# Transformer tower on one core: GpSimd adds two or three times in turn, VectorE sums eight or four numbers, and GpSimd scales the probabilities

## The reference, cut to what matters

```python
def one_query(qs):
    return -jnp.sum(jnp.abs(qs[:, None, :, :] - k), axis=-1) * scale   # sum over 64 numbers
...
a = _l1_scores(q, k)                                  # b x 128 x 128 x 8 heads
a = jnp.concatenate([a, jnp.zeros((b, 1, t, h), a.dtype)], axis=1)
a = jax.nn.softmax(a, axis=1)[:, :t]
bf = jnp.einsum('bsdh,bshw->bdhw', a, vf)
bb = jnp.einsum('bdsh,bshw->bdhw', a, vb)
```

## Time and profile before

| | |
|---|---|
| median of 3 runs | 3506.68 us |
| time of the profiled execution | 3508.91 us |
| its span | 3507.0 us |
| PE busy | 3243.3 us (92%) |
| DVE busy | 3086.9 us (88%) |
| POOL busy | 2856.5 us (81%) |
| ACT busy | 2723.1 us (78%) |
| DMA queue of GpSimd | 501.51 MB, 72.0% of 16 engines |

### The profile page before, as it was taken

How to read it: one execution, slowest core, us unless ns; L and a number is a source line. 1 busy time by engine, 2 the same in 40 slices (tenths; PEclk the granted TensorE clock), 3 DMA queues, 4 the chain that set the end, 5 groups by cost and what they waited for, 6 DMA issues and landing times. The chain is left out here.

```text
span 3507.0 us, 78749 instructions
## 1 busy us (share of the span) xinstructions
PE 3243.3 (92%) x23140; PEld 2458.9 (70%) x23140; DVE 3086.9 (88%) x4389; ACT 2723.1 (78%) x4859; POOL 2856.5 (81%) x2792
## 2 busy tenths in 40 slices
PE   8899999999999999999999999999999999999888
PEld 6676777776777777677767777766777777777555
DVE  5888889998898989988999889989989999989886
ACT  3777787887787877877788878778778788777875
POOL 2888888888888888888888888878888888888885
PEclk8999999999999999999999999999999999999999
DMA  6778777787787787777888877877777887778884
GB/s 135 154 153 164 155 155 153 157 162 156 151 163 154 157 161 158 158 150 153 161 160 159 160 153 156 164 149 157 157 155 157 166 159 157 154 158 160 163 159 86
DMA packets 199653, 543.63 MB, mean 155 GB/s; under 512 B 69142, under 2 KB 133398, under 8 KB 146744
## 3 DMA queue, kind: packets, MB, share of 16 engines
q0 software_dynamic: 73728, 501.51, 72.0%
q1 hardware_dynamic: 125880, 41.54, 5.9%
HBM read 10.93 MB, written 2.10 MB: 4 GB/s over the span
## 5 line engine op out<-in xcount | busy, mean ns | idle before, releaser
L925 DVE TENSOR_REDUCE S<-psU 128x16 f32<-128x1024 f32 x2183 | 2604.4, 1217 | 297.8 <-PE psU L486 281.3
L486 PE MATMUL psU<-flat,kT 99*128 99x256 bf16 x16384 | 2304.1, 275 | 212.5 <-ACT absd L711 102.9
L711 ACT ACTIVATE absd<-psU 128x1024 f32<-128x1024 f32 x1913 | 1936.7, 1023 | 554.3 <-PE psU L486 541.0
L486 PEld LDWEIGHTS psU<-flat,kT 99*128 99x128 bf16 x16384 | 1495.6, 98 | 855.2 <-DVE S L925 219.3
L1194 POOL TENSOR_TENSOR absd<-absd 128x1024 f32<-128x1024 f32 (+2 forms) x512 | 1179.8, 2304 | 248.9 <-DMA absd<-absd 245.0
L1198 POOL TENSOR_TENSOR absd<-absd 128x512 f32<-128x512 f32 (+2 forms) x512 | 610.3, 1192 | 40.2
L1183 POOL DMA_DIRECT2D absd<-absd x512 | 454.2, 887 | 200.4 <-ACT absd L711 145.2
L1201 POOL TENSOR_TENSOR absd<-absd 128x256 f32<-128x256 f32 (+2 forms) x512 | 351.7, 687 | 40.1
L498 PE MATMUL psC<-c1in,w 128*128 128x384 f32 (+1 forms) x930 | 309.4, 415 | 0.8 <-DVE c1in L969 0.8
L590 PE MATMUL psZ<-P,v 128*128 128x256 f32 x1024 | 288.6, 384 | 0.0
L517 PE MATMUL psC<-c3in,w 128*128 128x128 f32 x1240 | 251.8, 287 | 1.7 <-DVE c3in L969 1.7
(11 more groups left out here) (180 smaller groups left out, 2231.3 us busy)
## 6 DMA issues: line engine op xcount, KB each, us to landing
absd<-absd POOLq DMA_DIRECT2D x412, 1024.0 KB, 7.9
absd<-absd POOLq DMA_DIRECT2D x65, 768.0 KB, 6.5
flat<-qparts SPq DMA_DIRECT2D x3072, 8.0 KB, 4.1
absd<-absd POOLq DMA_DIRECT2D x35, 512.0 KB, 4.9
xin<-in_x SPq DMA_DIRECT2D x32, 192.0 KB, 8.0
flat<-pattern SPq DMA_DIRECT2D x4, 768.0 KB, 10.9
out_h<-result SPq DMA_DIRECT2D x32, 64.0 KB, 6.0
w<-in_w SPq DMA_DIRECT2D x1, 1280.0 KB
```

What stands on the lines that cost most here:

```text
L486: mm = nc.tensor.matmul(psU[:, slot % PLACES, m], kT[0:ROWS + 3, b, m, :], flat[0:ROWS + 3, half % HALVES, :, lo:lo + BLOCK], start=True, ...
L711: nc.scalar.activation(absd[:, c % GROUPS, :, u], psU[:, slot % PLACES].rearrange("p (n a) s w -> p n (a s w)", n=2), ACT.Abs).then_inc(a_ ...
L925: nc.vector.tensor_reduce(S[:, b, hd, SB * c:SB * c + SB], psU[:, slot % PLACES].rearrange("p a s w -> p s a w"), AX.XY, ALU.add, apply_ab ...
```

## The change

`LEVELS` becomes a list: even chunks keep three adds on GpSimd, odd chunks get two. `WIDTH` follows: VectorE's last adds of an odd chunk sum 8 numbers in place of 4. The waits on `a_tree` count the adds before a chunk (`LEVELS_BEFORE`). The eight scalings of an image leave ScalarE; in their place GpSimd has two `tensor_tensor` multiplications, each over four heads (512 numbers for each partition), with `rden` broadcast. They stand in the first slot and the middle slot of what the scalings had (`spread(..., 2)`): slots 100 and 103 for the first image, 29 and 35 for the second. The transposes wait for GpSimd's semaphore `at_pool`. `SHARED` and all slot tables stay as they are.

```diff
-LEVELS = 3
-WIDTH = 4
+LEVELS = [3, 2] * CHUNKS
+LEVELS_BEFORE = [sum(LEVELS[:c]) for c in range(TREES + 1)]
+WIDTH = [BLOCK >> (n - 1) for n in LEVELS]
...
+AT_POOL = Steps("scalea scaleb")
...
-                            pe.wait_ge(at_act, AT_ACT.after(g, ("scale3", "scale7")[n]))
+                            pe.wait_ge(at_pool, AT_POOL.after(g, ("scalea", "scaleb")[n]))
...
-                for n in spread(slot, AT_AT[b]["scale"], AT_AT[b]["scale_len"], HEADS):
-                    if n == 0:
-                        act.wait_ge(at_dve, AT_DVE.after(g, "rden"))
-                    nc.scalar.activation(P[:, n, 0, :], P[:, n, 0, :], ACT.Copy, scale=rden[:, n:n + 1]).then_inc(at_act, 1)
...
-                dve.wait_ge(a_tree, LEVELS * (TREES * i + slot // HEADS + 1))
+                dve.wait_ge(a_tree, LEVELS_BEFORE[TREES] * i + LEVELS_BEFORE[slot // HEADS + 1])
...
-                                        .rearrange("p u (s w) -> p u s w", w=BLOCK)[:, :, :, 0:WIDTH],
+                                        .rearrange("p u (s w) -> p u s w", w=BLOCK)[:, :, :, 0:WIDTH[slot // HEADS]],
...
-                pool.wait_ge(a_tree, LEVELS * (TREES * i + c) + 2)
-                lo, hi = rows[:, :, :, 0:WIDTH], rows[:, :, :, WIDTH:2 * WIDTH]
-                nc.gpsimd.tensor_tensor(lo, lo, hi, ALU.add).then_inc(a_tree, 1)
+                for k in range(1, LEVELS[c]):
+                    width = BLOCK >> k
+                    pool.wait_ge(a_tree, before + k)
+                    lo, hi = rows[:, :, :, 0:width], rows[:, :, :, width:2 * width]
+                    nc.gpsimd.tensor_tensor(lo, lo, hi, ALU.add).then_inc(a_tree, 1)
...
+            def attend(p, b, slot):
+                g = 2 * p + b
+                for n in spread(slot, AT_AT[b]["scale"], AT_AT[b]["scale_len"], 2):
+                    pool.wait_ge(at_dve, AT_DVE.after(g, "rden"))
+                    heads = slice(4 * n, 4 * n + 4)
+                    nc.gpsimd.tensor_tensor(P[:, heads, 0, :], P[:, heads, 0, :],
+                                            rden[:, heads].unsqueeze(2).broadcast_to([T, 4, T]), ALU.mult) \
+                        .then_inc(at_pool, 1)
```

More of the change, by code:

```diff
@@ L107 @@
 AT_PE = Steps("vf vb turna turnb pv")
-AT_ACT = Steps("vf vb exp0 exp1 exp2 exp3 exp4 exp5 exp6 exp7 scale0 scale1 scale2 scale3 scale4 scale5 scale6 scale7 turneda turnedb half tanh")
+AT_ACT = Steps("vf vb exp0 exp1 exp2 exp3 exp4 exp5 exp6 exp7 turneda turnedb half tanh")
+AT_POOL = Steps("scalea scaleb")
 AT_DVE = Steps("rden sum gate")
@@ L340, in vit_tower @@
         queries_pe, queries_act, queries_dve, queries_pool = (sem("queries_" + e) for e in ("pe", "act", "dve", "pool"))
-        at_pe, at_act, at_dve = (sem("at_" + e) for e in ("pe", "act", "dve"))
+        at_pe, at_act, at_dve, at_pool = (sem("at_" + e) for e in ("pe", "act", "dve", "pool"))
         ex_pe, ex_act, ex_dve, ex_pool = (sem("ex_" + e) for e in ("pe", "act", "dve", "pool"))
@@ L1192, in tree @@
                 pool.wait_ge(a_half[c % GROUPS], 16 * (TREES // GROUPS * i + c // GROUPS + 1))
+                before = LEVELS_BEFORE[TREES] * i + LEVELS_BEFORE[c]
                 lo, hi = absd[:, c % GROUPS, 0, 0:n, 0:SB * BLOCK], absd[:, c % GROUPS, 0, 0:n, SB * BLOCK:2 * SB * BLOCK]
@@ L1195, in tree @@
                 rows = lo.rearrange("p u (s w) -> p u s w", w=BLOCK)
-                pool.wait_ge(a_tree, LEVELS * (TREES * i + c) + 1)
-                lo, hi = rows[:, :, :, 0:8], rows[:, :, :, 8:16]
-                nc.gpsimd.tensor_tensor(lo, lo, hi, ALU.add).then_inc(a_tree, 1)
-                pool.wait_ge(a_tree, LEVELS * (TREES * i + c) + 2)
-                lo, hi = rows[:, :, :, 0:WIDTH], rows[:, :, :, WIDTH:2 * WIDTH]
-                nc.gpsimd.tensor_tensor(lo, lo, hi, ALU.add).then_inc(a_tree, 1)
+                for k in range(1, LEVELS[c]):
[3 more added lines that the diff above has]
+                    nc.gpsimd.tensor_tensor(lo, lo, hi, ALU.add).then_inc(a_tree, 1)
             def groups(i, slot, late):
@@ L1285, in iteration @@
                     groups(i, s, late)
+                    if late:
+                        attend(i - 1, 1, s)
                     kq(i, 1, s)
@@ L1290, in iteration @@
                         norm(i + 1, s)
+                    attend(i, 0, s - SECOND)
                     if ahead:
@@ L1300, in epilogue @@
                     tree(PAIRS - 1, s + SLOTS - TREE_AFTER)
+                    attend(PAIRS - 1, 1, s)
                     experts(PAIRS - 1, s)
```

## The result

| | before | after |
|---|---|---|
| median (lowest to highest), 20 runs each | 3505.17 us (3495.42 to 3514.65) | 3512.81 us (3502.69 to 3527.36) |
| profiled execution, its span | 3508.91, 3507.0 us | 3504.06, 3502.2 us |
| quiet pair in the profiled execution, median | 106.16 us | 105.95 us |

The changed kernel takes 1.0026 times as long as the one before, 95% interval 1.0014 to 1.0038: 7.6 us more. The profiled execution of after lies near the fast end of its kernel and is shorter than that of before, so the two traces put side by side don't show the loss. A "fall" is a stretch in which TensorE's granted clock was at its lower level, 1.2 in place of 2.4 GHz.

What follows compares the result with a forecast made beforehand. It saw no full engine but a chain changing hands within a pair, mostly between VectorE, TensorE and ScalarE. 9.3 + 2 - 0.3 + 4.4 = 15.4 us on 3508.9 gave 3524, as a median 3522 us; range 3484 to 3556.

Steps and rivals of the forecast that it cites:

- rival 4: TensorE's clock falls six more times in place of one, +22 us, 3544; or four fewer, -17; chance 0.08, half down.
- A sum of eight costs 0.27 us; chunks 13 and 3 pass whole: VectorE's longer last adds: 0.27 us each for chunks 13 and 3; 15, 1, 7, 5 nothing; all eight bounded 0 to 2.0.
- What is given back: Longer adds before VectorE's gaps (chunks 15, 1, 7, 5) cost nothing, TensorE or GpSimd being late there; no gain credited.
- The scalings leave ScalarE: -0.44, bounds 0.15 and 1.25: At the first image's scalings TensorE waits less for ScalarE, gaining 0.15 + 0.29 us a pair; second image nothing.
- 1.26 us for a multiplication: Each GpSimd scaling of 512 numbers taken as long as the nearest add, 1.26 us, 5.1 a pair; bounds 0.8 and 2.5.
- Rival 3: GpSimd scalings take 1.9 us, delaying second-image transposes and chunk 13's DMA: about 0.6 us a pair over forecast, 3540; chance 0.10.
- Chunk 13's DMA 1.5 us later: On GpSimd, first-image scalings and `qpart3` ahead of chunk 11's adds make chunk 13's DMA issue about 1.5 us later.
- `nmrn` 0.4 us late, at +0.20: GpSimd ends `nmrn` 0.4 us later, ScalarE waits, VectorE loses 0.20 us a pair; bounds 0 and 0.5.
- Last two passes +2, end -0.3: Without convolutions VectorE is late more often, +2 us; the run's final chain has one GpSimd add less, -0.3.
- One fall more, +4.4: Longer waits in TensorE's most-waiting slots, from chunk 13's add and `nmrn`, bring one more clock fall, costing 4.4 us.
- Rival 1: TensorE's waits for ScalarE at the first image vanish whole: -0.7 us a pair, -22 us, 3480 to 3485; chance 0.22.
- rival 2: VectorE is the bound; adds pass nearly whole: 1.6 to 2.0 us a pair, 3557 to 3569 us; chance 0.10.

Runs made afterwards that it cites:

- second_fewer: Changed kernel with the first image's scalings back on ScalarE and two GpSimd adds only in chunks 1, 5, 7, 11, 15: 3489.82 us, 0.9962 of before.
- levels_only: Changed kernel with all scalings back on ScalarE, so only the adds of odd chunks move to VectorE: 3495.20 us, 0.9961 of before.
- again_after: Changed kernel run once more, unedited, for a second trace: 3512.10 us, 1.0010 of before.
- c10_two: Changed kernel with two GpSimd adds in chunks 1, 5, 7, 10, 11, 13, 15 (chunk 10 in place of 3 and 9): 3483.24 us, 0.9940 of before.
- before_late: Kernel before with one GpSimd memset of 512 numbers into an unused tile in slot 4, delaying `nmrn`: 3542.80 us, 1.0108 of before.
- scale_only: Changed kernel with three GpSimd adds in every chunk, so only the scalings move to GpSimd: 3612.49 us, 1.0291 of before.
- c12_two: Changed kernel with two GpSimd adds in chunk 12 as well as the odd chunks: 3521.90 us, 1.0046 of before.

## Why the prediction was right in its side and wrong in its sum

The forecast was 3522 us and slower; 3512.8 was measured, slower and inside the range. But its sum was +11 us from longer pairs and +4.4 from the clock. Measured are -3 to -6 us from the pairs and +11 to +13 from the clock. The largest term has the wrong sign, and the one that decides is rival 4's. By the prediction's own last sentence it is wrong: the pair did get shorter. That the total came within 10 us is luck, of two errors that go against each other.

Cumulated from a pair's first unit, the quiet pairs of after stand against those of before like this (medians, us):

| at | slot 7 | 13 | 36 | 53 | 71 | 77 | 103 | 109 | 119 | end |
|---|---|---|---|---|---|---|---|---|---|---|
| after - before | +0.27 | +0.51 | +0.15 | +0.41 | +0.68 | +0.29 | +0.55 | +0.01 | -0.22 | -0.22 |

- *A sum of eight costs 0.27 us; chunks 13 and 3 pass whole.* The size held (677 ns), and both steps are in the table (slots 7 and 53). That chunk 5 costs nothing at its place was wrong: it is there (slot 71), and was given back later. Chunk 9's is there too (slot 103), ahead of the gap at the scalings that was to take it.
- *What is given back.* This step failed: only the scalings were credited with making the pair shorter. 0.36 us came back between slots 31 and 36, and the gap of 0.85 at 1057.23 in the earlier trace rows is gone. The prediction read TensorE as without a gap from 1044 to 1068, but in the very pair it read TensorE stands for the DMA of `flat`, a part of the queries, ahead of that unit, and VectorE waits for TensorE:

```profile
1056.59 0.61 PE L486 MATMUL psU<-flat,kT 99*128 99x256 bf16 x4 [0.35 <-DMA flat<-qparts]
```

After has no wait there in the pair shown:

```profile
1046.68 0.61 PE L488 MATMUL psU<-flat,kT 99*128 99x256 bf16 x4
```

TensorE stands more than 0.1 us ahead of this unit in 15 of the 28 middle pairs of before, in 4 of after's and in 2 of second_fewer's. Why the transfer is less often late isn't shown; that the fewer adds on GpSimd bring it is, since levels_only and second_fewer get 0.44 us back there. Another 0.39 came back at VectorE's wait for `rstdc`: 0.69 in the earlier trace rows, 0.40 in the row of after, and over the run 13.2 us in place of 21.9. Chunk 5's 0.27 is inside this. levels_only confirms both: all adds together cost 0 in the quiet pair, where 0.54 was put down (with bounds 0 and 2.0). In the sum of the pair, +0.30 forecast and -0.22 measured, the place at slot 36 is 0.36 of the difference of 0.52, and the one at `rstdc`, less chunk 5, 0.12.
- *The scalings leave ScalarE: -0.44, bounds 0.15 and 1.25.* Between slots 103 and 119 the table goes from +0.55 to -0.22, which is -0.77, or -0.51 with chunk 9's step counted in. That is near the value taken. TensorE's idle time of slots 103 to 109 fell from 1.09 to 0.21 us, and 0.61 in place of 0.16 came back at 109 to 119, now for VectorE. The gap of 0.42 is gone, as said.
- *1.26 us for a multiplication.* It is 1.11. The Trainium skill's estimate (page GPSIMD Engine Reference, section 3.1) of 1.1 us was right and the nearest row too high. Rival 3 needed 1.4.
- *Chunk 13's DMA 1.5 us later.* It is 0.43 later, counted from the reciprocal: 1016.39 - 1005.71 = 10.68 us before and, in the repeating pair, 1007.31 - 996.20 = 11.11 after. The first scaling fell into a wait that GpSimd had there anyway, for ScalarE, ahead of chunk 12's DMA.
- *`nmrn` 0.4 us late, at +0.20.* This held in size: slots 7 to 13 give +0.24. ScalarE waits in every pair, as said, but that alone was no sign of it, since levels_only has it without the cost. From the reciprocal, `nmrn` ends about as late as before (28.7 us and 28.6): the transfers of chunks 13 and 14 set it, and GpSimd waits for them. All the rest of the pair had come 0.5 us nearer.
- *Last two passes +2, end -0.3.* From the start of the last pass to its last unit it is 106.6 us before and 106.7 after. The +2 isn't there. From that unit to the end it is 31.8 and 31.6 us in the two traces of before and 29.8 in both of after: 1.7 to 1.9 less, where 0.3 less was put down.
- *One fall more, +4.4.* Mis-sized, and in both factors. The clock's mean share went from 0.9869 to 0.9814, 11 us. By the traces that is 1 to 6 falls more in the middle. And a fall of 10.24 us costs less than 4.4: in the seven pairs of again_after where it stands behind a late `nmrn` without more trouble, 2.9 to 3.1 us over the quiet pair. The pair that the prediction read is the fifteenth, whose long wait comes on top. It had the right stretch (chunk 13's add and `nmrn` where TensorE waits most) but too few falls. The rule of the Trainium skill (page TensorE: Matmul & The Clock Gate, Part 1) that the clock follows how busy the array has been agrees with where the falls of a trace lie, behind TensorE's longest waits. The total of its idle time doesn't order the kernels, though: levels_only has more of it between TensorE's slots 7 and 11 than before, 1.09 against 0.83 us in the median, and fewer falls in the middle (4 against 5). What was missed is how steep this is where the wait varies: 0.25 us more of it at this place is worth more than everything else in the sum.

- *The rivals.* Rival 1 needed a quiet pair of 105.6 us and rival 2 one of 107.7; by the same measure after has 105.95, between rival 1 and the 106.4 of the forecast. Rival 4's mechanism is what made the kernel slower, on top of a pair that is a little shorter.

That the late `nmrn` is the cause is shown from both sides: made late in the kernel before, it costs 38.6 us; with the first image's scalings taken off GpSimd in after, the loss becomes a gain of 10.9 us. And pair by pair: no fall began there behind a wait of under 0.65 us. What isn't shown is why the clock falls in one pair and not in another with the same waits: of 19 pairs of after with a late `nmrn` 6 had a fall, in the second trace 11 of 20.

## What to carry to other kernels

Where TensorE is nearly full and every engine is close behind, ask of each edit two things: what it does to the quiet stretch, and whether it makes a wait of TensorE longer right before the place where the clock already falls now and then. The second can be worth more, and one trace of each kernel doesn't show it, so compare the clock of many executions. Before an engine is given work, look for the small result it owes at the worst place (here `nmrn`, the last of four tiny instructions behind a tree), and make its room ahead of that place, as c10_two does.

## What the runs showed of the hardware that was not expected

- A few tenths of a us decide. With a median of 0.79 us of TensorE's idle time between slots 7 and 13 the clock fell in 5 of the 28 middle pairs of before, in both traces; with 1.04 us in 6 and 11 of after's; with 1.28 us in 17 of before_late's; and behind waits like the one of 2.49 us in all of scale_only's. By single pairs: none of 170 with under 0.65 us ahead of unit 11, 67 of 73 with over 1.2.
- Falls differ in length. Those in the middle of before lasted 10.24 us each, those of c12_two at slot 1 23.9 us. In the traces of before and after a middle pair with a fall took 108.9 to 112.1 us, with a long one of c12_two 113.7.
- A multiplication of 512 float32 numbers with a broadcast operand took GpSimd 1.11 us, an add of 512 in place 1.26, and a fill of 512 0.53.
